# First layer of a hybrid block: normalising the gate's rows and making their high parts on GpSimd instead of VectorE and ScalarE

## The reference

```
def _layernorm(x, axis=-1, eps=1e-05):
    m = jnp.mean(x, axis=axis, keepdims=True)
    v = jnp.var(x, axis=axis, keepdims=True)
    return (x - m) / jnp.sqrt(v + eps)
...
        B = jnp.power(1.0 - jnp.arccos(s) / jnp.pi, TAU)
        X = jnp.einsum('ni,ih->nh', B, q_weight)
        X = _l2_normalize(X) + bias
...
        logits = xf @ gate_w + gate_b
        top_w, top_i = jax.lax.top_k(logits, K)
        gw = jax.nn.softmax(top_w, axis=-1).astype(xf.dtype)
...
    x = x + _L0_attn_a_ref(_layernorm(x, axis=-1), L0_attn_a_ln_weight, L0_attn_a_ln_bias, L0_attn_a_k_weight, L0_attn_a_q_weight, L0_attn_a_bias)
    x = x + _L0_ffn_ref(_layernorm(x, axis=-1), L0_ffn_gate_w, L0_ffn_gate_b, L0_ffn_w1, L0_ffn_b1, L0_ffn_w2, L0_ffn_b2, L0_ffn_ws1, L0_ffn_bs1, L0_ffn_ws2, L0_ffn_bs2)
```

## Time and profile before

| | us |
|---|---|
| median of 3 runs | 634.68 (632.59 to 636.75) |
| the profiled execution, its own time | 635.94 |
| its span in the profile | 634.2 |
| VectorE busy in the span | 508.8 (80%) |
| TensorE busy (matmuls) | 483.8 (76%) |
| ScalarE busy | 454.5 (72%) |
| GpSimd busy | 371.9 (59%) |

### The profile page before, as it was taken

How to read it: one execution, slowest core, us unless ns; L and a number is a source line. 1 busy time by engine, 2 the same in 40 slices (tenths; PEclk the granted TensorE clock), 3 DMA queues, 4 the chain that set the end, 5 groups by cost and what they waited for, 6 DMA issues and landing times.

```text
span 634.2 us, 13564 instructions
## 1 busy us (share of the span) xinstructions
PE 483.8 (76%) x3827; PEld 358.1 (56%) x3827; DVE 508.8 (80%) x1181; ACT 454.5 (72%) x826; POOL 371.9 (59%) x391
## 2 busy tenths in 40 slices
PE   6788217774891988999677688875998879998770
PEld 6333017762440467888566577753444669997650
DVE  5899898888884448999788699876986479997992
ACT  2688995967592758999667577847797678997650
POOL 7000093337877778777667321147787777777673
PEclk9999858996796899999989999978999999999896
DMA  8810000004334644545741115101445435547943
GB/s 267 243 39 1 1 0 1 1 22 134 94 95 114 122 106 95 98 107 103 179 97 49 61 65 135 34 26 34 135 117 122 107 89 107 103 102 140 229 133 126
DMA packets 116798, 60.76 MB, mean 96 GB/s; under 512 B 81332, under 2 KB 105912, under 8 KB 116728
## 3 DMA queue, kind: packets, MB, share of 16 engines
q1 hardware_dynamic: 107640, 41.14, 28.6%
q0 software_dynamic: 9088, 18.76, 10.5%
HBM read 16.29 MB, written 23.90 MB: 63 GB/s over the span
## 4 chain that ended last, share of the span: by engine, by line
issue 25%; DVE 19%; SPq 18%; POOL 17%; PE 11%; ACT 6%; DMA 3%; POOLq 0%; DVEq 0%; ACTq 0%
POOL routed_rows L808 12%; SPq L630 11%; SPq L639 4%; SPq L628 2%; PE PA L1254 2%; DVE big L2160 2%; DMA side<-expert_results 2%; DVE side L2174 2%; ACT SC L1012 1%; PE PC L1472 1%; DVE BN L1492 1%; POOL RS L733 1%; DVE X L1697 1%; ACT big L1012 1%; DVE W L1620 1%
## 5 line engine op out<-in xcount | busy, mean ns | idle before, releaser
L857 POOL DMA_INDIRECT expert_results<-side,DG x156 | 163.1, 1046 | 58.6 <-issue 46.4
L808 POOL DMA_INDIRECT routed_rows<-big,SLQ x128 | 142.8, 1116 | 51.7 <-issue 39.4
L1472 PE MATMUL PC<-W,big 128*128 x624 | 119.0, 277 | 30.2 <-DVE side L2174 29.4
L1149 ACT ACTIVATE SC<-PA,B1T,scl 128x256 f32<-128x256 f32 x208 | 100.6, 573 | 16.4 <-PE PA L1456 12.1
L2163 DVE SCALAR_TENSOR_TENSOR big<-SC,scl,big 128x1024 f16<-128x1024 f32 x78 | 100.2, 1284 | 2.8
L1474 PE MATMUL PC<-W,big 128*128 x468 | 87.6, 222 | 0.0
L1472 PEld LDWEIGHTS PC<-W,big 128*128 128x128 f16 x624 | 58.5, 99 | 43.4 <-issue 35.6
L2160 DVE TENSOR_SCALAR big<-SC,scl 128x1024 f16<-128x1024 f32 x78 | 66.8, 856 | 5.9 <-ACT SC L1149 5.9
L1159 ACT ACTIVATE big<-PC,DG 128x128 f32<-128x128 f32 x156 | 49.8, 382 | 25.7 <-PE PC L1472 13.1
L733 POOL TENSOR_TENSOR RS<-VA,halfneg 128x4 f32<-128x4 f32 x24 | 25.3, 1055 | 64.5 <-DVE VA L1731 64.4
L2001 DVE SCALAR_TENSOR_TENSOR big<-SC,scl,big 128x1024 f16<-128x1024 f32 x32 | 41.0, 1282 | 25.2 <-ACT big L1119 24.8
(11 more groups left out here) (289 smaller groups left out, 1179.9 us busy)
## 6 DMA issues: line engine op xcount, KB each, us to landing
big<-PB SPq DMA_DIRECT2D x32, 256.0 KB, 3.3
side<-expert_results SPq DMA_DIRECT2D x16, 512.0 KB, 4.1
routed_rows<-pad_zeros SPq DMA_DIRECT2D x23, 128.0 KB
expert_results<-side,DG POOLq DMA_INDIRECT x156
X<-n_L_attn_a_hidden_states SPq DMA_DIRECT2D x2, 1024.0 KB, 7.0
W<-in_L_ffn_w SPq DMA_DIRECT2D x1, 2048.0 KB, 8.5
routed_rows<-big,SLQ POOLq DMA_INDIRECT x128, 2.6
out_x<-X SPq DMA_DIRECT2D x8, 256.0 KB
```

The costliest lines, as they stand in the source:

```text
L808: pool.indirect_dma_start(routed, bass.IndirectOffsetOnAxis(ap=SLQ[:, slot, t, c:c + 1], axis=0), XHL[:, slot, t, c, :].bitcast(I32), None ...
L857: pool.indirect_dma_start(results, bass.IndirectOffsetOnAxis(ap=DG[:, k, r, 0:1], axis=0), YT[:, k, r, :], None).then_inc(result_stored[k] ...
L1149: ins = act.activation(HF[:, k % 3, b * RU:(b + 1) * RU], up_out(k, b), ACT.Gelu, scale=INV1, bias=B1T[:, bass.ds(b1_at + b, 1)])
L1472: last = pe.matmul(both, hh, W2[:, :, at], start=(b == 0), stop=(b == HB - 1))
```

## The change

For groups 0 to 4 the normalising of the rows leaves VectorE and the high part leaves ScalarE. A new GpSimd part, `first_rows(g)`, does both: it waits for the root of its group, for the weight split to be done (the rows lie where the split's staging was) and for the slot, normalises with four instructions, waits for itself, and scales all four tiles into `XR` in one instruction. It stands in GpSimd's loop between the scale of the next group and the root of the next group. ScalarE's `gate_hi` stays for groups 5 to 7.

```
--- before.py
+++ after.py
@@ -796,6 +796,21 @@
                 power(RS[:, g * TPG:(g + 1) * TPG], VA[:, g * TPG:(g + 1) * TPG],
                       TPG).then_inc(s["root_made"], 1)
 
+            def first_rows(g):
+
+                pool.wait_ge(s["root_made"], norm_turn[1, g] + 1)
+                pool.wait_ge(s["w_split"], CHUNKS)
+                wait(pool, s["xl_ready"], g - 1)
+                rows_ = normal_rows(g, 0)
+                for t in range(TPG):
+                    at = g * TPG + t
+                    last = pool.tensor_scalar(rows_[:, t, :], X[:, at, :], MV[:, at, 0:1], RS[:, at:at + 1],
+                                              ALU.subtract, ALU.mult)
+                last.then_inc(s["g_xn"], 1)
+                pool.wait_ge(s["g_xn"], g + 1)
+                pool.tensor_scalar(XR[:, g * TPG:(g + 1) * TPG, 0:D], rows_, X_SCALE, None,
+                                   ALU.mult).then_inc(s["xh_ready"], 1)
+
             for layer in range(2):
                 def scatter(g, h, slot, tiles=range(TPG)):
 
@@ -836,6 +851,8 @@
                 else:
                     for g in range(NG - 2):
                         x_scale(g)
+                        if g:
+                            first_rows(g - 1)
                         group_root(g, 1)
                     x_scale(NG - 2)
                     scatter(0, 0, 0, (0,))
@@ -1083,7 +1100,7 @@
                     early_gelu(3)
                 else:
                     angle_log(0)
-                    straight(NG, [(2, value_squares), (-1, angle_log), (4, gate_turn), (3, gate_hi), (0, ninth)],
+                    straight(NG, [(2, value_squares), (-1, angle_log), (4, gate_turn), (0, ninth)],
                              until=NG)
                     value_squares(NG - 2)
                     gate_turn(NG - 4)
@@ -1819,18 +1836,6 @@
 
                 def first_shift(g):
                     shift(g, 1)
-
-                def first_normalise(g):
-                    if g >= ACT_NORMAL:
-                        return
-                    dve.wait_ge(s["root_made"], norm_turn[1, g] + 1)
-                    wait(dve, s["xl_ready"], g - 1)
-                    rows_ = normal_rows(g, 0)
-                    for t in range(TPG):
-                        at = g * TPG + t
-                        last = dve.tensor_scalar(rows_[:, t, :], tile_rows(at), MV[:, at, 0:1], RS[:, at:at + 1],
-                                                 ALU.subtract, ALU.mult)
-                    last.then_inc(s["g_xn"], 1)
 
                 def lo_part(g, h, k, half):
                     n = layer * NG + g
@@ -2117,7 +2122,7 @@
                     gate_logits(NG - 1)
                     early_split(3)
                 else:
-                    straight(NG, [(2, sum_squares), (3, first_normalise), (5, gate_logits), (2, add_values),
+                    straight(NG, [(2, sum_squares), (5, gate_logits), (2, add_values),
                                   (3, gate_lo), (2, first_moments)], until=NG)
                     gate_logits(NG - 5)
                     choose(0)
```

## The result

The changed kernel takes 651.46 us, the median of 4 runs (649.86 to 656.2); the kernel before, on the same chip, 634.01 (632.59 to 636.75). The ratio is 1.028 [1.021, 1.035]: slower by 17.45 us, where 7 were forecast and the range ended at 650. The profiled execution is the shortest of the four: 649.86 us, with a span of 648.1.

The account below looks back on a forecast made before the run. The bound was the first layer's value-stage wait chain through GpSimd and VectorE, 5.82 us a group. Period 4.54 + 2.68 = 7.22; five periods add 7.0 us to the median 634.68, about 642; range 636.5 to 650.

Parts of the forecast that it names:

- period = 4.54 + T: First layer's value stage: new time per group of 512 rows, 4.54 us plus T, forecast 7.22 instead of 5.82.
- break-even: Same loop: with T below 1.28 us the old path through the add returns and the period stays 5.82.
- T: GpSimd time added per group: four normalising instructions, a wait and a scaling, 4p + w + s = 2.68 us.
- The disturbance theory: Follow-up theory for the missing 10 us: VectorE's add or scalar reads disturb GpSimd, or the loop has another link.
- self-wait: The term w in T: GpSimd's wait on itself before the scaling, 0.08 us.
- p: One GpSimd normalising instruction on 128x128: taken as 0.45 us, near 0.40 read from a 1.65 us row with 1.25 blocking.
- s: GpSimd's scaling on 128x512: taken as 0.80 us, the middle between 0.61 from casts and 0.98 from a two-input add.
- rival 3: GpSimd loop: the add blocks, 647.3 us, or p is 1.65, 665.7 us; chance 0.11 together with Rival 4.
- Does the add disturb GpSimd: Add beside GpSimd's new work: no disturbance forecast, sum stays +7.0; were it to block, T 3.81 and +12.7 us.
- Rival 1: GpSimd's new instructions run at the cast's rate: T = 1.85, period 6.39, +2.9 us, 637.5; chance 0.27.
- Rival 4: TensorE's clock falls to 1.2 GHz: period 9.36, +17.7 us, 652.4; chance 0.11 together with rival 3.
- What is given back: Behind the loop, from the first scatter on: nothing returned; a length change over 2 us would prove the prediction wrong.

Follow-up runs that it names:

- the scaling alone: Against the changed kernel, normalising is back on VectorE and GpSimd only makes the high parts; 635.66 us against 633.74 before, ratio 1.0034.
- The constant form: Changed kernel with normalising by constants 0.0 and 1.0 instead of mean and root, and the scaling in four instructions; 652.73 us against 633.74 before, one run.
- the low part behind the moments: Changed kernel with VectorE making the low part after the next group's moments; 644.29 us against 633.74 before, ratio 1.0175.

## Why the prediction was wrong

**The bound and the loop: right.** The formula, period = 4.54 + T with a break-even at T = 1.28, holds where T was varied: 4.54 + 4.73 = 9.27 against 9.31 in the changed kernel, 6.12 against 6.15 with the scaling alone, and the old period but for 0.09 at T = 0.94. VectorE's removed instructions were worth nothing on the path, as said: the formula holds with them in the kernel with the scaling alone, and without them in the changed one. VectorE waits for GpSimd's scaling, as said. The disturbance theory falls as the main cause: no other engine held GpSimd up here, and no other link joined the loop; what is left of it is the read of the two scalars, 4 x 0.15 = 0.6 of the 2.05 us that T is above its forecast.

**The size of T: the step that failed.** T was put at 2.68 and measures 122.58 + 1.50 - 119.35 = 4.73. The self-wait was right (0.09 against 0.08). Both prices were wrong:

- p was 0.45 and is 0.785 in sequence (3.14 / 4): four of them make 1.34 us a group. The 0.40 was what GpSimd had left to do after the VectorE instruction beside it had ended, and the prediction took the 1.25 us ahead of that to be pure blocking. The constant form has since been measured undisturbed at 0.65 us, with one operation more than the instruction of the earlier trace rows; with one operation and an f16 result it lasts 0.53. So 0.13 to 0.25 us of work may have been done in the time that was counted as blocked; no run shows that instruction undisturbed. The remainder behind a disturbance is only a lower bound of the price, and was used as the price. The two scalars add about 0.15.
- s was 0.80 and is 1.50, outside both bounds, 0.61 and 0.98. The upper one came by the same subtraction: the two-input add on 128x512 lasts 1979 ns, and only the 0.98 us by which it prolonged its neighbour was taken as its own part. What the add itself showed, 1.98, would have been the upper bound; the 1.50 lies below it. The lower one came from casts, and a tensor_scalar doesn't follow their slope.

Put into the prediction's own formula the measured prices give 5 x (4.54 + 4 x 0.785 + 0.09 + 1.50 - 5.82) = 17.3 us, and the median grew by 17.45. The range failed with them: its upper end cut rival 3, in which p is the whole 1.65, at half of its chance, and had no case in which both prices are somewhat dearer at once.

**Does the add disturb GpSimd? No, as predicted.** The single normalising instructions of one group, from the timeline of GpSimd in the changed kernel, while the add runs from 119.38 to 120.50:

```profile
119.35 0.81 POOL L807 TENSOR_SCALAR side<-X,MV,RS 128x128 f32<-128x128 f32 x1
...
121.69 0.80 POOL L807 TENSOR_SCALAR side<-X,MV,RS 128x128 f32<-128x128 f32 x1
```

The first lies beside the add and the last has VectorE idle next to it; they last 0.81 and 0.80. The low part, with two inputs in SBUF, does disturb: the root beside it takes 1.53 in place of 1.02 in the kernel with the low part behind the moments. The Trainium skill ("SBUF — State Buffer", Who interferes with whom) says that a VectorE instruction with two SBUF inputs contends with a GpSimd instruction that reads SBUF, and that one with at most one, outside the two-port modes, does not. The traces agree on both sides.

**Rival 1, the cast's rate: not so.** The Trainium skill ("GPSIMD Engine Reference", 4.1 Engine selection) calls one-input work on GpSimd roughly line-rate; here the one-input scaling took 2.53 ns an element, against 0.82 for the casts. The measurement decides: by the prediction's estimate from that rate the kernel would be at 637.5, and it is at 651.46.

**Rival 4, TensorE's clock: its condition came, its price didn't.** The timeline of TensorE in the changed kernel, and in the second fence four windows (us, busy of PE, PEld, DVE, ACT, POOL, granted clock, DMA, GB/s):

```profile
115.55 1.04 PE L1328 MATMUL PB<-identh,PB 128*128 128x128 f16 x8 [4.01 <-DVE PB L1843]
...
116.38 6.02 PE L1253 MATMUL PC<-QW,big 128*128 128x128 f32 x32
...
124.86 1.04 PE L1328 MATMUL PB<-identh,PB 128*128 128x128 f16 x8 [2.46 <-DVE PB L1843]
...
126.16 6.26 PE L1253 MATMUL PC<-QW,big 128*128 128x128 f32 x32
...
134.17 0.62 PE L1328 MATMUL PB<-identh,PB 128*128 128x128 f16 x8 [1.75 <-DVE PB L1843]
...
135.03 3.82 PE L1253 MATMUL PC<-QW,big 128*128 128x128 f32 x32
...
143.48 1.03 PE L1328 MATMUL PB<-identh,PB 128*128 128x128 f16 x8 [4.63 <-DVE PB L1843]
```

```profile
116.00:119.00 3.00, 3.00 (x18) 3.00 (x17) 1.42 (x8) 2.37 (x2) 1.94 (x3) 0.50 0.00 0
126.00:129.00 3.00, 3.00 (x25) 3.00 (x23) 1.23 (x5) 2.76 (x2) 2.63 (x4) 0.50 0.02 5
136.00:139.00 3.00, 2.85 (x26) 2.66 (x24) 1.27 (x6) 1.77 (x2) 2.91 (x5) 1.00 0.00 0
145.00:148.00 3.00, 3.00 (x15) 3.00 (x16) 1.27 (x5) 2.37 (x2) 2.91 (x4) 0.50 0.02 5
```

After idle stretches of 4.01 and 4.63 us the granted clock was 0.50, the 1.2 GHz level, and so it was again in the group behind the first of them; the value matmuls of these three groups took 5.52 to 6.26 us in place of 3.82. But the new period of 9.31 has room for them: TensorE is idle for 1.75 to 4.63 us before it turns the rows of each group all the same, and the wait ends with the low part each time. Groups at the low and at the full clock have the same period of 9.31. That rival 4 had forecast a period of 9.36 and 652.4 us, next to the measured 9.31 and 651.46, is chance: even the slowest group kept TensorE for no more than 126.16 + 6.26 - 124.86 = 7.56 us, and the 9.31 adds up from GpSimd's and VectorE's rows.

**What is given back: nothing that can be shown.** The prediction wanted the stretch from the first scatter to the end within 2 us of before; in the profiled execution it is 648.1 - 163.29 = 484.8 in place of 634.2 - 145.99 = 488.2, shorter by 3.4. That test was too sharp: over the nine profiled executions of this study, one of each kernel, the stretch lies between 483.9 and 489.2 and doesn't follow the length of the loop. The medians show nothing returned, to within their interval of about 4 us either way: +17.45 for a loop that is 17.4 longer.

## What to carry to other kernels

Two things must be known before work is moved onto a waiting engine: the loop that the move closes, and the price of this very form of instruction on that engine undisturbed. The first could be read from the trace of before to a few hundredths; the second couldn't, and then the whole duration of the nearest row is the upper end, never what is left after subtracting a neighbour. An engine that is idle within a loop offers only its slack in that loop (1.28 us here), however low its busy share of the span. Another order of the instructions can widen that slack, and then the same move can pay there, though here the whole was not shown to beat the kernel before.

## What the runs showed of the hardware

- GpSimd's tensor_scalar from f32 to f16 took 0.53, 0.86 and 1.50 us at 128, 256 and 512 elements a partition: 0.21 us and 2.53 ns an element. The two-operation form on 128 elements took 0.65 with constants and 0.80 with two scalars from memory, where VectorE makes four such rows in 1.11.
- Two scalars per partition from memory cost about 0.15 us an instruction on GpSimd.
- The same normalising instruction lasted as long beside VectorE's add as with VectorE idle (0.81 and 0.80), while a root beside the two-input low part lasted half as long again (1.53 against 1.02).
